# A transformer block of eight batches on one core: a new timetable of filler units and row work, another order of the last batch, and attention output in other PSUM banks

## The chip, the cores and the metric

The kernel runs on one core of a Trainium2 chip. The metric is the device time of one execution in microseconds (us). Three runs of the kernel before gave a median of 995.27 us (992.34 to 995.49).

## The reference

The input x is 8 batches of 512 rows with 256 columns, in fp32. The block does, for each batch:

```
h = layernorm(x) * (1 + ca) + sa                 # ca, sa, ga, sb, cb, gb come from silu(c) @ wmod
x = x + ga * attention(h)
h = layernorm(x) * (1 + cb) + sb
x = x + gb * ffn(h)

attention(h) = light + heavy
light: second layernorm, q, k, v = xl @ wqkv; 8 heads of 64; windows of 64 rows that look at
       themselves and both neighbours; softmax; @ wo_l
heavy: two routers (h @ rt_q, h @ rt_kv) sort the rows; the last 256 of each order are kept;
       rms norm; q = . @ wq_h, k, v = . @ wkv_h; full softmax attention 256 x 256; @ wo_h;
       its rows are set back at the places that the first router picked
ffn(h): y = relu(h @ W_fc^T)^2 @ W_proj^T; five steps of a spiking neuron on y; mean of the spikes
```

## The kernel before, in words

**Slots.** A batch is an iteration of 24 slots. Slots 0 to 15 are light attention, four head pairs p times four row tiles m (s = 4p + m). Slots 16 to 23 are heavy attention, four head pairs times two query tiles. Each slot handles two heads and 128 query rows. Slots are numbered through: n = 24 b + s. The pipeline of one n goes over three engines, written out by hand, and each engine works through them strictly in its written order:

- TensorE in slot n (lines 1094 to 1102): `scores(n+2)`, the slot's filler units, `turn(n)` (six or eight 64-row transposes of the normalized probabilities, line 1053), `attend(n-1)` (the product with v, lines 1074, 1079, 1089).
- VectorE in slot n: `copy_out(n-2)` (line 1323, it evicts the output of attend and adds its two halves; below this is called the eviction), `invert(n+1)` (reciprocal of the row sums, line 1316), `minimum(n+2)` (lines 1306 to 1310), the units' share, then the row work that the function `stages` puts into that slot.
- ScalarE in slot n: `copy_pT(n-1)` (lines 847, 851), `exp_step(n+2)` (line 829), the units' share, `normalize(n+1)` (line 839).

`scores(n+3)` waits for exp of n+2. The attend's output `ps_oT` is columns 256 to 383 of the two banks whose columns 0 to 255 hold the scores (`ps_scores`). Therefore `attend(n-1)` waits for exp of n+2 as well, and `copy_out(n-2)` waits until the scores n+2 are written:

```
ps_oT = ps_scores[:, :, SEL:SEL + P]
pe.wait_ge(exp_ready, min(n + 4, SLOTS * B))       # attend(n)
dve.wait_ge(scores_ready, min(n + 5, SLOTS * B))   # copy_out(n)
```

**Filler units.** The products that aren't attention are cut into units and given to slots by the table `SLOT_UNITS`. HT transposes the routed rows (ScalarE makes the high part, VectorE the low part, line 1342, and frees the bank); Q, K, V, HQ, HK, HV are projections (line 895; fp32 is split in two parts, so there are six matmuls a unit); NQ, NK, NV are those of the next batch; LO (line 943) and HO (line 948) are the two output projections; ZT and Z3 are transposes of normed rows (lines 953, 958); FC and YA (lines 895, 1006) are the feed-forward layer; SR and RK turn the router's scores and count ranks (lines 973 to 982). Units of all kinds but YA use the two banks `ps_unit` in turn, so a unit waits until the one before the last is drained. Heavy output HO, Z3, FC, YA and the neuron work on the batch before: in iteration b they belong to batch b-1.

**Row work on VectorE** (`stages`): statistics and norms of batch b+1 (`stats1`, `center`, `modulate`, `stats2`, `router_scores`, `second_norm`, `compare`), `add_rows`, `stats3`, `third_norm` and ten neuron steps of batch b-1. GpSimd makes reciprocal roots (`rstd1` to `rstd3`), the rms norm (`norm_rows`), the low part of the squares of FC (`square_low`), scatters rows in router order to DRAM (line 619), gathers the heavy output back (line 639), adds x to LO (`add_x`) and ends a batch with `final`. SyncE loads and stores in one fixed order; each of its transfers waits behind all that it issued before.

**The last batch.** Iteration 7 has no next batch to prepare. Its heavy slots come last as in all others, so HO of batch 7, the store of its rows, the gather, `add_rows`, `stats3`, `third_norm`, Z3 and the whole feed-forward layer stand behind them in a segment "tail", which works in two halves of 256 rows.

## Time and profile before

| | |
|---|---|
| median of three runs | 995.27 us |
| the profiled execution | 1000.88 us, with a span of 999.1 us from first to last instruction |
| mean granted TensorE clock | 0.930 of full speed |
| TensorE matmul busy | 855.5 us (86% of the span), 8914 instructions |
| VectorE busy | 556.6 us (56%) |
| ScalarE busy | 583.5 us (58%) |
| GpSimd busy | 396.5 us (40%) |
| starts of slot 0, iterations 0 to 7 | 54.7, 167.1, 276.6, 389.2, 502.0, 614.5, 727.3, 839.8 us |
| chain that ended last | PE 59%, DVE 22%, ACT 8%, issue 6% |

In the profile PE is TensorE, DVE VectorE, ACT ScalarE, POOL GpSimd, SP SyncE. PEclk is the granted TensorE clock as a share of 2.4 GHz; it has two levels, 1.00 and 0.50 (1.2 GHz). L1323 is line 1323 of the kernel.

### The profile page before, as it was taken

Reading aid. Unit: us, or ns where it says so; the run is one execution under the profiler, and the core shown is the slowest. Engines: PE = TensorE matmul, PEld = TensorE weight load, DVE = VectorE, ACT = ScalarE, POOL = GpSimd, SP = SyncE. Lnnn points to the kernel's source line nnn. Section 1 sums busy time; section 2 is a strip of 40 time slices with the busy share of each in tenths; the row PEclk is TensorE's granted clock in tenths of the full one; section 3 lists DMA queues with packets and bytes.
Section 4 is the critical chain, followed back from the end, with each engine's and each line's share of the span. In section 5 each row is a group of like instructions: output and inputs, shape, how many; then the busy total and the mean of one; then the engine's idle time right before and its main releaser. Section 6 shows DMA issues by size and latency. Waiting matters only on the chain.

```text
span 999.1 us, 23412 instructions
## 1 busy us (share of the span) xinstructions
PE 855.5 (86%) x8914; PEld 654.3 (65%) x8914; DVE 556.6 (56%) x1602; ACT 583.5 (58%) x1682; POOL 396.5 (40%) x437
## 2 busy tenths in 40 slices
PE   5758599799988999799988999799988999899655
PEld 2436466577756876577756876577756876587455
DVE  7645634764557554764557554764557554614344
ACT  1156556576656765676656765576556765676332
POOL 3322031375424542365424543365424542252243
PEclk9878779999999999999999999999999999999768
DMA  8220002100210012200220012200220011200100
GB/s 314 67 80 2 27 28 70 59 2 23 80 59 23 2 38 85 59 2 19 71 73 23 1 39 85 60 2 17 72 73 22 3 38 54 59 2 2 37 22 22
DMA packets 32479, 45.33 MB, mean 45 GB/s; under 512 B 3928, under 2 KB 26720, under 8 KB 32368
## 3 DMA queue, kind: packets, MB, share of 16 engines
q1 hardware_dynamic: 26944, 31.24, 9.8%
q0 software_dynamic: 4608, 12.59, 3.8%
q8 instruction: 72, 1.18, 0.5%
q14 instruction: 39, 0.32, 0.1%
q10 hardware_dynamic: 816, 0.00, 0.0%
HBM read 28.85 MB, written 14.97 MB: 44 GB/s over the span
## 4 chain that ended last, share of the span: by engine, by line
PE 59%; DVE 22%; ACT 8%; issue 6%; DMA 2%; POOL 2%; SPq 0%; DVEq 0%; POOLq 0%; ACTq 0%
PE ps_unit L895 25%; PE ps_y L1006 7%; PE ps_unit L943 6%; ACT probs L829 5%; PE ps_unit L948 4%; PE ps_turned L1053 4%; PE ps_scores L1089 3%; PE ps_scores L1074 3%; DVE row_min L1306 3%; PE ps_scores L1038 3%; PE ps_scores L1029 3%; DVE loT L1323 2%; ACT hT L794 1%; DVE bn L1268 1%; DMA late<-in_L_wmod 1%
## 5 line engine op out<-in xcount | busy, mean ns | idle before, releaser
L829 ACT ACTIVATE probs<-ps_scores,row_min 128x192 f32<-128x192 f32 (+2 forms) x384 | 161.3, 425 | 182.8 <-DVE row_min L1306 125.6
L839 ACT ACTIVATE probs<-probs,row_inv 128x192 f32<-128x192 f32 (+2 forms) x384 | 155.7, 458 | 0.0
L1323 DVE TENSOR_REDUCE loT<-ps_scores 128x128 f32<-128x256 f32 x128 | 53.5, 418 | 141.3 <-PE ps_scores L1029 92.0
L895 PE MATMUL ps_unit<-xT,wfcT 128*128 128x512 f32 (+1 forms) x432 | 112.8, 404 | 9.4 <-DVE xT L1247 8.8
L895 PE MATMUL ps_unit<-xT,wqkv 128*128 128x512 f32 x384 | 109.6, 422 | 3.3 <-POOL xT L653 3.3
L1006 PEld LDWEIGHTS ps_y<-wprojT,hid_parts 128*128 128x128 f32 x768 | 99.3, 190 | 9.9 <-issue 6.0
L432 POOL TENSOR_TENSOR hid<-hid 128x512 f32<-128x512 f32 (+1 forms) x64 | 63.5, 992 | 106.4 <-ACT hid L807 105.1
L1006 PE MATMUL ps_y<-wprojT,hid_parts 128*128 128x256 f32 x768 | 104.6, 284 | 0.2
L895 PEld LDWEIGHTS ps_unit<-xT,wfcT 128*128 128x128 f32 x432 | 78.6, 206 | 33.4 <-issue 20.2
L578 POOL TENSOR_SCALAR veps<-mv 128x4 f32<-128x4 f32 (+1 forms) x25 | 5.1, 202 | 227.7 <-DVE mv L1166 133.1
L1074 PE MATMUL ps_scores<-probsT,v 64*64 64x128 f32 x1024 | 58.7, 299 | 38.9 <-ACT probs L829 38.6
L1053 PEld LDWEIGHTS ps_turned<-ident,probs 64*128 64x128 f32 x1280 | 55.6, 140 | 54.9 <-issue 44.3
L895 PEld LDWEIGHTS ps_unit<-xT,wqkv 128*128 128x128 f32 x384 | 71.3, 193 | 24.3 <-issue 10.2
L436 POOL TENSOR_TENSOR hid_parts<-hid,hid_parts 128x512 fp32r<-128x512 f32 (+1 forms) x64 | 79.2, 1237 | 13.4 <-ACT hid_parts L811 11.2
L1053 PE MATMUL ps_turned<-ident,probs 64*128 64x64 f32 x1280 | 82.2, 241 | 1.9 <-ACT probsT L851 1.7
L619 POOL DMA_INDIRECT sorted_rows<-hn,rank x64 | 64.4, 1006 | 45.7 <-DVE rank L1350 33.0
L847 ACT ACTIVATE probsT<-ps_turned 128x384 f32<-128x384 f32 x128 | 61.9, 484 | 33.6 <-PE ps_scores L1079 33.3
L1306 DVE TENSOR_REDUCE row_min<-ps_scores 128x2 f32<-128x512 f32 (+1 forms) x128 | 77.1, 602 | 2.5 <-PE ps_scores L1029 2.5
L1323 DVE TENSOR_REDUCE late<-ps_scores 128x128 f32<-128x256 f32 x64 | 27.0, 422 | 88.0 <-PE ps_scores L1038 44.8
L829 ACT ACTIVATION_READ_ACCUMULATOR probs<-ps_scores,row_min 128x1 f32 x384 | 75.3, 196 | 0.0
L1029 PE MATMUL ps_scores<-kT,qT 64*64 64x192 f32 (+1 forms) x1024 | 71.8, 317 | 3.3 <-ACT probs L829 3.3
L943 PE MATMUL ps_unit<-wo_light,loT 128*128 128x256 f32 x256 | 63.8, 392 | 0.0
(158 smaller groups left out, 1690.9 us busy)
## 6 DMA issues: line engine op xcount, KB each, us to landing
xa<-in_L_attn_x SPq DMA_DIRECT2D x8, 512.0 KB, 5.0
routed<-sorted_rows SPq DMA_DIRECT2D x16, 256.0 KB, 3.0
lx<-in_L_attn_x SPq DMA_DIRECT2D x8, 512.0 KB, 3.8
...
sorted_rows<-hn,rank POOLq DMA_INDIRECT x64, 2.4
...
```

What stands on the lines that cost most here:

```text
L436: eng.tensor_tensor(hid_parts[1][:, i % 2, cols], square, hid_parts[0][:, i % 2, cols].bitcast(F32), ALU.subtract).then_inc(low, 1)
L619: pool.indirect_dma_start(out=sorted_rows[r], out_offset=bass.IndirectOffsetOnAxis(ap=rank[:, r, t:t + 1], axis=0), in_=hn[:, t, :], in_of ...
L829: ins = act.activation(probs[:, probs_buffer(s), probs_columns(s, part)], ps_scores[:, part, lo:hi], ACT.Exp, bias=row_min[:, s % 3, part: ...
L839: ins = act.activation(rows, rows, ACT.Identity, scale=row_inv[:, s % 3, part:part + 1])
L895: ins = pe.matmul(ps, w(wi, k, w_cols), a(ai, k, a_cols), start=(n == 0), stop=(n == 3 * KD - 1))
L943: ins = pe.matmul(ps[:, 0:D], loT[:, p, i * P:(i + 1) * P], wo_light[:, p, :], start=(p == 0), stop=(p == PAIRS - 1))
L1006: ins = pe.matmul(ps_y[t // 2][:, (t % 2) * D:(t % 2 + 1) * D], hid_parts[hi][:, i % 2, t * P:(t + 1) * P], wprojT[wi][:, f, :], start=(f ...
L1029: ins = pe.matmul(ps_scores[c * W:(c + 1) * W, w, lo:hi], qT[heads[h], p % 2, query:query + W], kT[heads[h], p % 2, first_key + lo:first_k ...
L1053: ins = pe.transpose(ps_pT[:, c, i * W:(i + 1) * W], probs[rows, probs_buffer(s), run * P:(run + 1) * P], ident[rows, rows])
L1074: ins = pe.matmul(ps_oT[halves[h], g ^ h, :], v[halves[g], m, cols[h]], both, start=True, stop=m == (T - 1, 0)[g])
L1306: ins = dve.tensor_reduce(row_min[:, s % 3, :], ps_scores[:, :, lo:hi], AX.X, ALU.min)
L1323: dve.tensor_reduce(dst[:, p, m * P:(m + 1) * P], ps_oT.rearrange("p g n -> p n g"), AX.X, ALU.add).then_inc(oT_copied, 1)
```

## The change

It does six things.

1. `ps_oT` moves to columns 256 to 383 of the banks of the turned probabilities (`ps_turned`). `attend` no longer waits for exp. `turn(n)` waits for the eviction of n-2, and the eviction of n waits until the turned probabilities of n+1 are copied. Each row half of attend writes one bank (`g` in place of `g ^ h`).
2. On VectorE the eviction moves behind `invert` and `minimum`.
3. `SLOT_UNITS` is written anew. K(1) moves from the end of the iteration before to slot 0, LO(3) to slot 4 of the next iteration, and SyncE waits for it before gate_a is loaded anew.
4. The row work gets other slots, some of it in two parts (`stats1`, `center`, `stats3`), and the neuron steps go from slots 17 to 20 to slots 20 to 23. GpSimd's steps move with them.
5. Buffers of probabilities and row sums are taken by n, not by s.
6. The last batch has its own order of slots (`LAST_ORDER`) and units (`LAST_UNITS`): light pairs 0 and 1, all heavy slots, then pairs 2 and 3 by row tile. Its heavy output (HX), light output (LX 0, 1), store and gather come inside the iteration, LX(2), LX(3) at the start of the tail.

```diff
 SLOT_UNITS = {
-    0: [("HT", 0), ("V", 3)],
-    1: [("HO", 0), ("HO", 1)],
-    2: [("HT", 1), ("Q", 2)],
-    3: [("HV", 1)],
-    4: [("K", 2)],
+    0: [("HT", 0), ("K", 1), ("HT", 1)],
+    1: [("V", 3), ("HO", 0)],
+    2: [("HO", 1)],
+    3: [("Q", 2)],
+    4: [("K", 2), ("LO", 3)],
     5: [("Q", 3)],
     6: [("K", 3)],
-    7: [("HV", 0), ("Z3", 0), ("Z3", 1)],
-    8: [("FC", 0), ("FC", 1)],
-    9: [("HQ", 0), ("FC", 2), ("YA", 0)],
-    10: [("FC", 3), ("YA", 1), ("SR", 0)],
-    11: [("FC", 4), ("YA", 2)],
-    12: [("FC", 5), ("YA", 3), ("HK", 0)],
-    13: [("RK", 0), ("FC", 6), ("YA", 4), ("SR", 1)],
-    14: [("FC", 7), ("YA", 5)],
-    15: [("YA", 6), ("ZT", 0)],
-    16: [("YA", 7), ("ZT", 1), ("RK", 1)],
-    17: [("HQ", 1), ("HK", 1)],
-    18: [("LO", 0), ("NQ", 0)],
-    19: [("LO", 1), ("NK", 0)],
-    20: [("LO", 2), ("NV", 0)],
-    21: [("LO", 3), ("NQ", 1)],
-    22: [("NV", 1), ("NK", 1)],
-    23: [("NV", 2)],
+    7: [("HV", 1)],
+    8: [("HV", 0)],
+    9: [("Z3", 0), ("Z3", 1), ("HQ", 0)],
+    10: [("HK", 0), ("FC", 0)],
+    11: [("FC", 1), ("SR", 0)],
+    12: [("FC", 2), ("YA", 0)],
+    13: [("FC", 3), ("YA", 1)],
+    14: [("FC", 4), ("YA", 2), ("RK", 0), ("SR", 1)],
+    15: [("FC", 5), ("YA", 3)],
+    16: [("HQ", 1), ("FC", 6), ("YA", 4)],
+    17: [("HK", 1), ("FC", 7), ("YA", 5)],
+    18: [("YA", 6), ("ZT", 0), ("ZT", 1), ("RK", 1)],
+    19: [("YA", 7), ("NQ", 0)],
+    20: [("NK", 0), ("NV", 0)],
+    21: [("LO", 0), ("NV", 1)],
+    22: [("LO", 1), ("NQ", 1)],
+    23: [("LO", 2), ("NV", 2)],
 }
+LAST_ORDER = [*range(LIGHT // 2), *range(LIGHT, SLOTS)] + [p * T + m for m in range(T) for p in (2, 3)]
+LAST_UNITS = {
+    0: [("HT", 0), ("K", 1), ("HT", 1)],
+    1: [("V", 3), ("HO", 0), ("HO", 1)],
+    2: [("HQ", 0)],
+    3: [("HK", 0), ("LO", 3)],
+    4: [("HV", 1)],
+    5: [("HQ", 1)],
+    6: [("HK", 1)],
+    7: [("HV", 0)],
+    8: [("Z3", 0), ("Z3", 1)],
+    9: [("FC", 0), ("Q", 2)],
...
+    18: [("HX", 0), ("HX", 1)],
+    19: [("YA", 6), ("YA", 7)],
+    20: [("LX", 0)],
+    22: [("LX", 1)],
+}
...
-        ps_oT = ps_scores[:, :, SEL:SEL + P]
         ps_turned = ctx.enter_context(nc.psum_tensor("ps_turned", [P, 2, 512], F32))
         ps_pT = ps_turned[:, :, 0:SEL]
+        ps_oT = ps_turned[:, :, SEL:SEL + P]
...
                 pe.wait_ge(probs_ready, n + 1)
-                if not (isinstance(n, int) and n == 0):
+                if n > 0:
                     pe.wait_ge(pT_copied, n)
+                if n > 1:
+                    pe.wait_ge(oT_copied, n - 1)
...
                 if n > 0:
                     pe.wait_ge(oT_copied, n)
-                pe.wait_ge(exp_ready, min(n + 4, SLOTS * B))
...
                 dve.wait_ge(oT_ready, n + 1)
-                dve.wait_ge(scores_ready, min(n + 5, SLOTS * B))
+                dve.wait_ge(pT_copied, min(n + 2, SLOTS * B))
...
-            NEURON = {17: [(0, 1), (0, 2)], 18: [(0, 3), (0, 4), (0, 5)], 19: [(1, 1), (1, 2)],
-                      20: [(1, 3), (1, 4), (1, 5)]}
+            NEURON = {20: [(0, 1), (0, 2)], 21: [(0, 3), (0, 4)], 22: [(0, 5), (1, 1), (1, 2)],
+                      23: [(1, 3), (1, 4), (1, 5)]}
...
                 if not first:
-                    if s == 5:
                     if s == 6:
+                        add_rows(b - 1)
+                        stats3(b - 1, tiles=range(1))
+                    if s == 7:
+                        stats3(b - 1, tiles=range(1, T))
+                    if s == 8:
                         third_norm(b - 1)
...
+                if s == 1:
+                    stats1(b + 1, range(2))
+                if s == 2:
+                    stats1(b + 1, range(2, T))
+                if s in (3, 4):
+                    center(b + 1, range(2 * (s - 3), 2 * (s - 2)))
+                if s == 5:
+                    modulate(b + 1)
+                if s == 10:
+                    stats2(b + 1)
+                    router_scores(b + 1, 0)
+                if s == 11:
+                    router_scores(b + 1, 1)
+                if s in (12, 13):
+                    compare(segment, b + 1, 0, range(2 * (s - 12), 2 * (s - 11)))
+                if s == 14:
+                    second_norm(b + 1)
+                if s in (15, 16):
+                    compare(segment, b + 1, 1, range(2 * (s - 15), 2 * (s - 14)))
...
-                        copy_out(n - 2, (s - 2) % SLOTS)
-                    if not (last and s + 1 >= SLOTS):
-                        invert(n + 1, (s + 1) % SLOTS)
-                    if not (last and s + 2 >= SLOTS):
-                        minimum(n + 2, (s + 2) % SLOTS)
+                        copy_out(n - 2, slot_at(s - 2, last))
...
-            attend("tail", B, SLOTS * B - 1, SLOTS - 1)
+            unit("tail", B, ("LX", 2))
+            attend("tail", B, SLOTS * B - 1, LIGHT - 1)
```

On GpSimd `rstd1` goes from slot 2 to 3, `rstd3` from 5 to 7, `rstd2` from 7 to 10, `norm_rows` from 8 to 11, the scatters from slots 14 to 20 to slots 15 to 21, and the first half of `final` from slot 20 to 23.

## Rows read from the trace of the kernel before

**Rows 1.** Busy time by stretch: two whole iterations; columns stand in the first line.

```profile
core 0: us, PE busy (x) PEld busy (x) DVE busy (x) ACT busy (x) POOL busy (x), PEclk, DMA share, GB/s
167.10:276.60 109.50, 99.77 (x1109) 77.24 (x1105) 66.50 (x193) 70.86 (x207) 50.10 (x53) 0.98 0.13 42
389.20:501.90 112.70, 102.70 (x1110) 79.33 (x1104) 66.53 (x193) 70.79 (x207) 50.35 (x53) 0.95 0.13 40
```

**Rows 2.** Same view, iteration 3: slots 0, 1, 2-8, 9-15, 16-17, 18-23.

```profile
389.20:392.50 3.30, 3.30 (x52) 2.41 (x45) 0.95 (x3) 2.29 (x9) 0.00 (x0) 1.00 0.03 5
392.50:400.50 8.00, 6.42 (x50) 4.85 (x44) 3.27 (x10) 2.61 (x10) 0.00 (x0) 0.79 0.00 0
400.50:431.00 30.50, 23.85 (x266) 16.54 (x261) 22.56 (x77) 18.95 (x58) 11.61 (x17) 0.94 0.17 49
431.00:463.80 32.80, 32.78 (x383) 27.44 (x379) 17.92 (x54) 23.83 (x68) 21.25 (x20) 1.00 0.01 2
463.80:475.50 11.70, 10.14 (x138) 8.80 (x131) 6.77 (x16) 6.77 (x19) 6.55 (x6) 0.85 0.13 46
475.50:501.90 26.40, 26.22 (x274) 19.28 (x270) 15.06 (x34) 16.35 (x48) 10.94 (x11) 1.00 0.29 91
```

**Rows 3.** Same view: slot 1 of iteration 3, and of iteration 1.

```profile
394.90:398.30 3.40, 3.40 (x10) 2.69 (x9) 0.30 (x2) 1.54 (x6) 0.00 (x0) 0.50 0.00 0
169.60:173.10 3.50, 1.93 (x34) 1.50 (x34) 2.33 (x7) 2.10 (x7) 0.00 (x0) 1.00 0.00 0
```

**Rows 4.** Who waited for whom, whole span: us in total, times, longest.

```profile
ACT probs L829 <- DVE row_min L1306: 125.6, 128, 2.8
PE ps_scores L1074 <- ACT probs L829: 38.6, 47, 2.1
```

**Rows 5.** Timeline of slots 0 and 1, iteration 3: start, length, instruction, idle before.

```profile
391.67 0.83 ACT L794 ACTIVATE hT<-ps_unit,gamma_cols 128x256 fp32r<-128x256 f32 x2
392.62 0.87 DVE L1342 SCALAR_TENSOR_TENSOR hT<-ps_unit,gamma_cols,hT 128x256 fp32r<-128x256 f32 x2 [1.79 <-ACT hT L794]
...
394.57 5.38 PE L948 MATMUL ps_unit<-wo_heavy,late 128*128 128x256 f32 x16 [1.58 <-DVE late L1323]
```

**Rows 6.** Busy time by stretch: slot 5 of iteration 3, one unit.

```profile
412.20:415.20 3.00, 2.81 (x43) 1.88 (x36) 2.44 (x7) 2.41 (x10) 0.00 (x0) 1.00 0.00 0
```

**Rows 7.** Costliest groups: the eviction of attention output.

```profile
L1323 DVE TENSOR_REDUCE loT<-ps_scores 128x128 f32<-128x256 f32 x128 | 53.5, 418 | 141.3 <-PE ps_scores L1029 92.0
```

**Rows 8.** Timeline, VectorE, slot 20 of iteration 3: a v copy, three neuron steps.

```profile
488.97 0.69 DVE L1337 COPY v<-ps_unit 128x512 f32<-128x512 f32 x1 [0.98 <-PE ps_unit L895]
489.58 2.13 DVE L1298 SCALAR_TENSOR_TENSOR spikes<-ps_y,spikes 128x512 f32<-128x512 f32 x3
```

**Rows 9.** Timeline of slot 7, iteration 3: Z3 on TensorE and ScalarE.

```profile
423.31 0.66 PE L958 MATMUL ps_unit<-ident,hn 128*128 128x128 f32 x4 [1.55 <-DVE v_r L1337]
...
424.00 0.78 ACT L778 ACTIVATE full<-ps_unit,shift_b,scale_b 128x512 f32<-128x512 f32 x1 [1.43 <-PE ps_unit L958]
```

**Rows 10.** second_norm: all instructions (ns, least/median/most), and those of iteration 3.

```profile
L1216 DVE TENSOR_SCALAR xa<-h,mv,rstd x32: 399/406/1508, 19.5 to 778.8; 128x256 f32<-128x256 f32 x32
...
438.18 3.20 DVE L1216 TENSOR_SCALAR xa<-h,mv,rstd 128x256 f32<-128x256 f32 x4
```

**Rows 11.** DMA issues: count, KB each, median us from issue to landing.

```profile
xa<-in_L_attn_x SPq DMA_DIRECT2D x8, 512.0 KB, 5.0
```

**Rows 12.** Busy time by stretch: slots 8 to 16 of iteration 0.

```profile
90.00:133.50 43.50, 29.23 (x372) 21.51 (x368) 26.58 (x88) 25.15 (x76) 9.09 (x13) 0.75 0.06 20
```

**Rows 13.** By stretch: iteration 7, the way to FC; timeline: Z3 and FC there.

```profile
839.80:936.70 96.90, 87.39 (x997) 66.60 (x986) 41.48 (x116) 64.25 (x189) 31.79 (x31) 0.97 0.08 23
936.70:961.20 24.50, 8.50 (x38) 6.27 (x37) 7.79 (x22) 1.62 (x3) 5.74 (x8) 0.57 0.11 35
...
958.32 1.09 PE L958 MATMUL ps_unit<-ident,hn 128*128 128x128 f32 x4 [12.82 <-DVE hn L1281]
...
961.18 4.04 PE L895 MATMUL ps_unit<-xT,wfcT 128*128 128x256 f32 x18 [1.77 <-DVE xT L1247]
```

More of the change, by code:

```diff
@@ L95, in slot_units, with slot_at @@
 def slot_units(slot, first, last):
[L97 to L98 removed]
+    if last:
+        return LAST_UNITS.get(slot, [])
+    units = [u for u in SLOT_UNITS[slot] if not (first and u in EARLIER_UNITS)]
     return units + FIRST_UNITS.get(slot, []) if first else units
+def slot_at(position, last):
+    return LAST_ORDER[position] if last and 0 <= position < SLOTS else position % SLOTS
 def iteration_units(first, last):
@@ L712, in _ @@
             iteration("last", B - 1, last=True)
-            gather(B - 1, True, in_tail=True)
-            for half in range(2):
-                rstd3(B - 1, half)
+            rstd3(B - 1, 0)
+            add_x("tail", B, ("LX", 2))
+            add_x("tail", B, ("LX", 3))
+            rstd3(B - 1, 1)
             for u in SEGMENTS["tail"]:
-                unit("tail", B, u)
+                if u[0] != "LX":
+                    unit("tail", B, u)
             final(pool, B - 1, 0)
```

256 lines of the change are left out of this document (146 added, 110 removed).

## The prediction

> **What bounds the kernel now.** I read the table by iteration first [rows 1]: how long each is, how much of it TensorE works, at what clock. Iteration 3 lasts 112.7 us, TensorE is busy 102.7 of it, and its granted clock is 0.95; iteration 1 lasts 109.5 with 99.8 busy at 0.98. Iterations 2 to 6 are alike within 0.3 us. The stretches of iteration 3 [rows 2] show where the idle 10.0 us lie: none in slot 0, 1.6 in slot 1, 6.65 in slots 2 to 8, 1.6 in slots 16 and 17, next to none in 9 to 15 and 18 to 23. The clock column there names the second loss: 0.79, 0.94 and 0.85 in the stretches with holes, 1.00 elsewhere. Each is one fall to 1.2 GHz of 3.4 us, as in the first of [rows 3]; the second row there is the same place of iteration 1, where a hole as long brought none. Two falls more cost 102.7 - 99.8 = 2.9 us of busy time, 1.5 each, so a full-clock iteration holds 98.3 us of TensorE work.
>
> The waits [rows 4] name what opens the holes. In a slot VectorE evicts the output of slot n-2, takes the row minimum of n+2, ScalarE makes exp of it, and attend(n-1) waits for that exp, as its output shares the scores' banks: 38.6 us in 47 waits, behind the 125.6 that exp waits for the minimum. The hole of slot 1 is another [rows 5]: HT(0) goes through ScalarE (0.83) and VectorE (0.87, after 1.79 idle) and the eviction that HO(0) needs is queued behind it; TensorE waits 1.58. A slot with one projection is 3.0 us, 2.8 of them work [rows 6]. My split of that 2.8 is 1.3 for the projection and 1.5 for scores, turn and attend; a heavy slot's three take about 1.7. Slots 18 to 23 then leave 26.2 - 7 x 1.3 - 6 x 1.7 = 6.9 for four LO: 1.7 an output unit. All three are estimates from these rows.
>
> **The change, part by part.** *Output into the turned banks.* The attend's wait for exp goes. In its place turn(n) waits for eviction n-2, which VectorE now makes behind the minimum. Scores wait for exp and exp for the minimum, so this loop is one eviction (0.42) [rows 7] shorter: about 0.5 scores, 0.6 minimum, 0.9 exp and gaps, 2.3 us in all. A slot with one unit has 2.84 us of TensorE work, hence it becomes bound by TensorE, if VectorE is on time. The eviction ends 1.6 us after the slot starts and turn comes at 1.8 to 2.0; covered by 0.2 us only. Where VectorE is late, turn is late by the same.
>
> *Timetable of the loop.* Units and VectorE work are the same; TensorE's 98.3 us stay. I walked the new slots, each engine in its order, with the durations above. Slots 1 to 7 come out without holes: every one has a unit, and row work is at most 1.7 us a slot. Four places do not.
> - Slot 0: HT(0), K(1), HT(1), where HT(1) wants the bank of HT(0). VectorE ends slot 23 late: NV(2) is filled 3.6 us into it, the copy takes 0.7, three neuron steps 2.1 [rows 8], so 6.5 against a slot of 4.6. Minimum 0.6, exp 0.8, HT(0) on ScalarE 0.85 and on VectorE 0.9 follow: HT(0)'s bank is free 5.1 us into slot 0, TensorE has had nothing since 2.3. Idle 2.9 with the gaps.
> - Slot 8: HV(1)'s copy and three statistics end 0.9 late, so minimum, eviction and turn: 0.6.
> - Slot 9: Z3 waits for the third norm (0.75), then HQ(0) wants the bank of Z3(0), drained behind exp by a 0.78 activation, as today's 1.55 [rows 9]: 1.35. Together 2.1.
> - Slots 10 and 11: second statistics 1.9 and the router's sums, which GpSimd stretches. Today second_norm, four instructions with a median of 406 ns, takes 3.20 beside GpSimd's squares [rows 10]. So two slots of 4.1 and 3.3 get up to 6 us of VectorE each: 1.0. (The Trainium skill, "SBUF — State Buffer", section Who interferes with whom, says that a VectorE instruction with two SBUF inputs, or in two-port mode, and GpSimd lock each other out for a whole instruction. The trace agrees; by it alone the price would be 0 or 2 as the overlap falls.)
> The rest 0.4. Sum 7.0 against 10.0. The hole before slot 17 closes, as RK(1) has two slots more: no fall there. The holes of slots 0 and 9 are at least as long as those that bring falls today, so two stay, 3.0 us. (The Trainium skill, "TensorE: Matmul & The Clock Gate", section HAM oscillation, tells of falls behind waits for transfers; by its rule holes as short as these would do no harm. Here 1.58 did, so the trace decides; by the page the loop would be 105.3.) A new iteration: 98.3 + 7.0 + 3.0 = 108.3. Six now take 109.5 + 5 x 112.64 = 672.7, then 649.8: **-22.9**.
>
> Transfers move too. final() of the second half now runs on GpSimd 1.9 to 4.4 us into slot 0, and SyncE's store and the load of xa are queued behind it; with 5.0 to land [rows 11] xa comes 10.0 in, the statistics start at 10.8. Cost 0, but 0.8 us of cover; if it goes, the minimum of slot 2 waits, up to 2 us. The gather ends some 22 us in, GpSimd's save_rank and add_x(LO 3) behind it at 23.5, before add_rows at 25. Scatter of the second list ends in slot 21, reload lands 2.6 us before HT(0). All at nothing, bounds 0 and 2 us an iteration for the three.
>
> *First iteration.* 43.5 us of slots 8 to 16 hold 29.2 of TensorE work at a clock of 0.75 [rows 12]: VectorE and the chain bound it. HV(1) leaves slot 3, where its weights are barely made, LO(3) leaves (1.7), K(1) comes behind HT(0). Bounds 0 and -10; I take **-5**, nearer to the moved units' own price than to the idle.
>
> *Last batch.* To its last attend but one it takes 96.9 us, then 24.5 to FC(0) [rows 13]. In those 24.5 TensorE sits 12.8 idle behind HO, store, gather and norm; the row of Z3 shows it, and FC starts at 961.2. Heavy pairs now come before the last eight light slots: HX in slot 18, gather in 19, all below LX and attention. Left behind that attend: LX(2) 1.7, attend 0.7, eviction 0.5, LX(3) 1.7, Z3 0.6, its three steps 2.1 and gaps of 0.4: 7.7. The iteration itself gains the old batch's LO(3), two HX and K(1) and loses its own LO(2) and LO(3): 3 x 1.7 + 1.3 - 2 x 1.7 = 3.0 us, to 99.9. 121.4 - 107.6 = 13.8: **-14**. Bounds -3 (gather late after all) and -17.
>
> Sum -22.9 - 5 - 14 = -42. The profiled execution took 1000.9 (span 999.1 and 1.8 around it), so 958.9; the median shown is 5.6 lower: 953.
>
> **Rivals.**
> *B, holes closed.* ScalarE or VectorE is quicker than I walked, idle 5.5 and no fall: 103.8 an iteration, -49.9 -5 -14: 926. For: the 2.3 us loop, and iteration 1's hole without a fall. Against: the order in slot 0 is fixed by bank and queue. The clock page's rule ends near here, at 935.
> *C, holes only move.* The waits of turn on late evictions eat the rest and three falls stay: loop 112.6, tail -14 and first -5: 976. For: 0.2 us of cover. Against: idle 6.65 in slots 2 to 8 comes from a wait that goes.
> *D, slower.* Each turn waits a full eviction, since VectorE is a slot behind: 0.42 [rows 7] x 190 slots = +80, 953 + 80 = 1033. It needs the wait in more than half of the slots (over 42 us). Against: VectorE is busy 59% of an iteration, and in 12 slots two units cover it.
> *E, the last batch gives nothing* because its gather still ends late: 967.
>
> **How the numbers follow.** A 0.50, B 0.17, C 0.20, E 0.06, D 0.07. The likeliest gives 953. The range runs from 926 (B) to 979 (C and its 3 us), leaving out D and the outer half of B. About 0.3% (3 us) is what a measurement here can tell from none: faster 0.91, same 0.02, slower 0.07.
>
> **What would show it.** Right: attend waits for no exp, 2 to 7 have no idle TensorE, HT(1) waits 2 to 3 us on VectorE, falls in slots 1 and 10 alone, FC of the tail starts within 9 us of the last attend but one. Wrong: turn waiting for VectorE in many slots, xa awaited by VectorE in slot 1, or three falls.

## The result, and the profile after

The changed kernel takes **970.87 us** (median of 4 runs, 969.66 to 971.63); the kernel before, run beside it, 995.38 us (992.34 to 1001.5). The ratio is 0.9745, 95% interval 0.9698 to 0.9792: faster by 2.5%. The forecast was 953.0 us in a range of 926 to 979. The sign and the range hold; the gain is 24.5 us and not 42.

Busy time by stretch, changed kernel: iterations 1 and 3 (columns as in [rows 1]); of iteration 4, slots 0, 1, 2-7, 8-9, 14 and 15; and after the last "..." the last iteration from slot 0 to the end of the last attend but one, and from there to FC(0):

```profile
core 0: us, PE busy (x) PEld busy (x) DVE busy (x) ACT busy (x) POOL busy (x), PEclk, DMA share, GB/s
159.90:265.30 105.40, 100.14 (x1113) 76.81 (x1106) 68.20 (x191) 71.36 (x206) 45.01 (x50) 0.98 0.10 30
375.30:484.40 109.10, 101.41 (x1110) 77.59 (x1104) 70.65 (x194) 71.47 (x206) 49.20 (x54) 0.97 0.13 43
484.40:492.10 7.70, 5.01 (x56) 3.66 (x51) 4.02 (x9) 4.07 (x12) 4.19 (x4) 0.82 0.34 101
492.10:496.70 4.60, 4.60 (x40) 3.30 (x36) 2.60 (x9) 2.23 (x8) 0.00 (x0) 0.93 0.51 149
496.70:515.40 18.70, 18.70 (x233) 13.18 (x229) 13.77 (x43) 14.09 (x46) 6.11 (x8) 1.00 0.22 68
515.40:524.30 8.90, 6.52 (x86) 4.85 (x80) 7.22 (x25) 5.13 (x15) 1.23 (x2) 1.00 0.07 25
...
540.50:548.40 7.90, 6.11 (x84) 4.90 (x80) 6.34 (x13) 5.17 (x14) 5.17 (x5) 0.93 0.00 0
548.40:553.80 5.40, 5.40 (x64) 4.07 (x60) 2.67 (x9) 2.88 (x9) 1.72 (x2) 0.78 0.02 5
...
812.30:916.60 104.30, 93.64 (x1013) 72.37 (x1005) 45.59 (x121) 65.66 (x189) 37.05 (x36) 0.93 0.10 29
916.60:931.20 14.60, 8.07 (x35) 5.90 (x33) 7.58 (x21) 1.62 (x3) 6.74 (x9) 0.73 0.15 45
```

Read it against [rows 1, 2]. Iteration 3 is 3.6 us shorter and its idle is 7.7 us where it was 10.0. In iteration 4 slots 2 to 7 are full: 18.70 busy of 18.70, where slots 2 to 8 left 6.65 us open. What is idle now stands mostly in three places: slot 0 (2.7), slots 8 and 9 (2.4) and slot 14 (1.8). The clock column is below 1 in slots 0-1 and 14-15: two falls to 1.2 GHz of 3.4 us in this iteration, in place of three. The six iterations aren't alike: iteration 1 has 5.3 us of idle and one fall, iteration 2 has three falls and takes 110.1 us, iteration 3 has one fall of 6.8 us, and 4 to 6 have two of 3.4. The last two lines answer to [rows 13].

The waits of the whole span and the eviction's group (columns as in [rows 4] and [rows 7]):

```profile
ACT probs L885 <- DVE row_min L1377: 80.9, 100, 3.5
...
PE ps_turned L1114 <- DVE loT L1394: 16.3, 18, 2.6
```

```profile
L1088 PE MATMUL ps_scores<-kT,qT 64*64 64x192 f32 (+1 forms) x1024 | 73.6, 330 | 3.3 <-ACT probs L885 3.3
L1394 DVE TENSOR_REDUCE loT<-ps_turned 128x128 f32<-128x256 f32 x128 | 53.3, 416 | 10.5 <-ACT probsT L903 9.3
```

Attend's wait for exp, 38.6 us in 47 waits in [rows 4], is gone. The 3.3 us in the row of L1088 are the scores' own wait for exp, which the kernel before has with the same 3.3. In the place of attend's wait stands turn's wait for the eviction, 16.3 us in 18 waits, none of them over 0.5 us in the six loop iterations: 0.48 in slot 8 and 0.38 in slot 13. Before it evicts light output VectorE is idle 10.5 us in all, 9.3 of it for ScalarE's copy of the turned probabilities; before heavy output it waits 0.2 us for it.

By stretches of the span, with the forecast beside them (starts of slots 0 from the first scores of each iteration):

| stretch | before | after | difference | forecast |
|---|---|---|---|---|
| start and first iteration | 167.1 | 159.9 | -7.2 | -5 |
| six loop iterations | 672.7 | 652.3 | -20.4 | -22.9 |
| last iteration and tail | 159.3 | 157.6 | -1.7 | -14 |
| span | 999.1 | 969.8 | -29.3 | -42 |

The profiled run of the kernel before was 5.6 us above its median, that of the changed kernel 0.8 above its own; so 29.3 us of span are 24.5 of median. In the first row 1.6 us lie ahead of slot 0 of iteration 0 (54.66 and 53.04 us) and 5.5 in iteration 0; no run takes these apart.

Slot 0 of iteration 4, in the timeline, answers to [rows 5]:

```profile
485.28 1.65 PE L951 MATMUL ps_unit<-xT,wqkv 128*128 128x512 f32 x6
...
486.29 0.15 DVE L1387 RECIPROCAL row_inv<-row_sum 128x2 f32<-128x2 f32 x1
...
487.74 0.84 ACT L850 ACTIVATE hT<-ps_unit,gamma_cols 128x256 fp32r<-128x256 f32 x2
...
488.69 0.88 DVE L1413 SCALAR_TENSOR_TENSOR hT<-ps_unit,gamma_cols,hT 128x256 fp32r<-128x256 f32 x2 [1.46 <-ACT hT L850]
489.58 0.47 SPq L570 DMA_DIRECT2D xa<-in_L_attn_x  x1
489.62 1.11 PE L980 MATMUL ps_unit<-ident,routed 128*128 128x128 f32 x4 [2.69 <-DVE hT L1413]
```

This is the hole that was forecast. The slot starts at 484.4; VectorE is free of the neuron steps 1.9 us in, HT(0)'s bank is free 5.2 us in (forecast 5.1), and TensorE waits 2.69 us (forecast 2.9 with its gaps).

Slot 14, same view:

```profile
541.60 0.34 DVE L1300 SCALAR_TENSOR_TENSOR late<-late,score,later 128x128 bf16<-128x128 f32 x1
...
542.91 1.35 POOL L481 TENSOR_TENSOR hid_parts<-hid,hid_parts 128x512 fp32r<-128x512 f32 x1
543.04 1.37 DVE L1300 SCALAR_TENSOR_TENSOR late<-late,score,later 128x128 bf16<-128x128 f32 x1
...
544.41 0.67 DVE L1377 TENSOR_REDUCE row_min<-ps_scores 128x2 f32<-128x512 f32 x1
...
545.11 0.47 ACT L885 ACTIVATE probs<-ps_scores,row_min 128x256 f32<-128x256 f32 x1 [2.59 <-DVE row_min L1377]
...
546.02 0.59 ACT L863 ACTIVATE hid<-ps_unit 128x512 f32<-128x512 f32 x1
...
546.67 0.65 PE L1030 MATMUL ps_unit<-ident,score 128*128 128x128 f32 x4 [1.48 <-ACT hid L863]
```

This hole was not forecast. The same instruction of the router's comparison takes 0.34 us at 541.60 and 1.37 us at 543.04, where it starts 0.13 us behind a GpSimd product of 1.35 (the low part of the squares) and ends 0.15 us behind it. So the minimum comes late, exp behind it, and ScalarE drains FC(4)'s bank only behind exp; SR(1) wants that bank. Delays of the kind that I priced in slots 10 and 11 are real, and stand in slots 13 and 14. (The rule of the Trainium skill, "SBUF — State Buffer", section Who interferes with whom, that the prediction tells, agrees with this pair of rows: VectorE's instruction, which started second, ends just behind GpSimd's.)

The way to FC(0) in the last batch, same view:

```profile
908.55 1.40 DVE L1369 SCALAR_TENSOR_TENSOR spikes<-ps_y,spikes 128x512 f32<-128x512 f32 x2
...
908.78 0.40 PE L1114 MATMUL ps_turned<-ident,probs 64*128 64x64 f32 x6 [2.37 <-DVE loT L1394]
...
916.54 3.37 PE L1000 MATMUL ps_unit<-wo_light,loT 128*128 128x256 f32 x8
...
921.32 1.08 DVE L1352 TENSOR_SCALAR hn<-h,mv,rstd 128x256 f32<-128x256 f32 x2 [0.94 <-POOL rstd L627]
922.33 0.41 DVE L1394 TENSOR_REDUCE loT<-ps_turned 128x128 f32<-128x256 f32 x1
922.88 3.60 PE L1000 MATMUL ps_unit<-wo_light,loT 128*128 128x256 f32 x8 [2.48 <-DVE loT L1394]
...
928.57 0.75 DVE L1337 BATCH_NORM_STATS2 bn<-h 128x6 f32<-128x256 f32 x2
...
931.18 1.20 PE L951 MATMUL ps_unit<-xT,wfcT 128*128 128x256 f32 x4 [3.75 <-DVE xT L1313]
```

The gather's wait of 12.82 us is gone, as forecast. But each thing that TensorE still needs is now behind row work on VectorE: the evictions stand behind neuron steps and behind the third norm, which itself waits for GpSimd, and the parts of xT that FC(0) reads stand behind the sums and statistics of the other half. Between these waits the clock falls, and LX(2) and LX(3) take 3.37 and 3.60 us each where run 9's LX(2) takes 1.99 at full clock.

### The profile page after: what moved, and what is told of

Same layout as the page of the kernel before. It is cut to its first block, busy times and chain, and to the rows that moved or that the text cites. A ratio compares the mean times of both kernels' runs of the same rounds, so it can differ in the third digit from the quotient of the medians.

```text
span 969.8 us, 23414 instructions
## 1 busy us (share of the span) xinstructions
PE 853.9 (88%) x8914; PEld 648.3 (67%) x8914; DVE 584.6 (60%) x1602; ACT 589.6 (61%) x1682; POOL 391.0 (40%) x437
## 4 chain that ended last, share of the span: by engine, by line
PE 64%; DVE 19%; ACT 7%; issue 4%; POOL 2%; DMA 2%; SPq 0%; DVEq 0%; ACTq 0%; POOLq 0%
PE ps_unit L951 26%; PE ps_y L1063 7%; PE ps_unit L1000 6%; PE ps_turned L1114 5%; PE ps_turned L1149 4%; PE ps_turned L1134 3%; PE ps_unit L1005 3%; PE ps_scores L1088 3%; PE ps_scores L1097 3%; ACT probs L885 2%; DVE late L1300 2%; DVE late L1297 2%; DVE routed L1273 1%; DVE late L1299 1%; DVE spikes L1369 1%
## 5 line engine op out<-in xcount | busy, mean ns | idle before, releaser
L885 ACT ACTIVATE probs<-ps_scores,row_min 128x192 f32<-128x192 f32 (+2 forms) x384 | 161.7, 426 | 126.2 <-DVE row_min L1377 80.9
L951 PE MATMUL ps_unit<-xT,wqkv 128*128 128x512 f32 x384 | 112.5, 431 | 3.8 <-POOL xT L702 3.8
L1063 PEld LDWEIGHTS ps_y<-wprojT,hid_parts 128*128 128x128 f32 x768 | 99.9, 191 | 9.3 <-issue 5.5
L1114 PEld LDWEIGHTS ps_turned<-ident,probs 64*128 64x128 f32 x1280 | 57.6, 144 | 71.2 <-issue 61.1
L1114 PE MATMUL ps_turned<-ident,probs 64*128 64x64 f32 x1280 | 84.3, 245 | 17.5 <-DVE loT L1394 16.3
L951 PE MATMUL ps_unit<-xT,wfcT 128*128 128x512 f32 (+1 forms) x384 | 95.7, 387 | 4.3 <-DVE xT L1313 3.7
L951 PEld LDWEIGHTS ps_unit<-xT,wfcT 128*128 128x128 f32 x384 | 66.3, 200 | 24.8 <-issue 13.6
L1088 PE MATMUL ps_scores<-kT,qT 64*64 64x192 f32 (+1 forms) x1024 | 73.6, 330 | 3.3 <-ACT probs L885 3.3
L1000 PE MATMUL ps_unit<-wo_light,loT 128*128 128x256 f32 x256 | 67.3, 409 | 2.5 <-DVE loT L1394 2.5
L712 POOL TENSOR_TENSOR lx<-lx,hid 128x256 f32<-128x256 f32 x28 | 20.5, 732 | 102.9 <-DVE hid L1429 102.9
L1134 PE MATMUL ps_turned<-probsT,v 64*64 64x128 f32 x1024 | 60.4, 308 | 0.0
L1000 PEld LDWEIGHTS ps_unit<-wo_light,loT 128*128 128x128 f32 x256 | 49.5, 202 | 16.3 <-issue 9.5
```

The source lines that it names most:

```text
L885: ins = act.activation(probs[:, probs_buffer(n), probs_columns(s, part)], ps_scores[:, part, lo:hi], ACT.Exp, bias=row_min[:, n % 3, part: ...
L951: ins = pe.matmul(ps, w(wi, k, w_cols), a(ai, k, a_cols), start=(n == 0), stop=(n == 3 * KD - 1))
L1000: ins = pe.matmul(ps[:, 0:D], loT[:, p, i * P:(i + 1) * P], wo_light[:, p, :], start=(p == 0), stop=(p == PAIRS - 1))
L1063: ins = pe.matmul(ps_y[t // 2][:, (t % 2) * D:(t % 2 + 1) * D], hid_parts[hi][:, i % 2, t * P:(t + 1) * P], wprojT[wi][:, f, :], start=(f ...
L1088: ins = pe.matmul(ps_scores[c * W:(c + 1) * W, w, lo:hi], qT[heads[h], p % 2, query:query + W], kT[heads[h], p % 2, first_key + lo:first_k ...
L1114: ins = pe.transpose(ps_pT[:, c, i * W:(i + 1) * W], probs[rows, probs_buffer(n), run * P:(run + 1) * P], ident[rows, rows])
```

## The experiments

Twelve kernels ran in three jobs, each beside the kernel before. Each job had another chip, so what differs between jobs may belong to the chip. Ratios are against the kernel before of the same job, with 95% intervals. Loop means the six iterations 1 to 6, end means from the last iteration's slot 0 to the end of the span, both in the profiled execution.

| run | edit | median us | ratio | loop | end |
|---|---|---|---|---|---|
| 1 | bank move alone | 965.93 | 0.9703 (0.9679-0.9727) | 647.3 | 157.3 |
| 2 | the rest, old banks | 978.21 | 0.9822 (0.9793-0.985) | 656.0 | 156.8 |
| 3 | old last batch | 971.64 | 0.9767 (0.9742-0.9793) | 653.3 | 157.1 |
| 4 | HT(1) in slot 2 | 962.71 | 0.9674 (0.9651-0.9698) | 642.2 | 157.1 |
| 5 | norm_rows in slot 14 | 970.46 | 0.9725 (0.967-0.978) | 650.6 | 158.6 |
| 6 | SR(1) in slot 15 | 966.54 | 0.9693 (0.9645-0.9741) | 648.0 | 158.6 |
| 7 | eviction first | 1020.23 | 1.0225 (1.0165-1.0284) | 687.4 | 163.6 |
| 8 | last order on VectorE | 977.12 | 0.9786 (0.9732-0.9841) | 668.0 | 154.5 |
| 9 | changed kernel again | 986.2 | 0.9864 (0.983-0.9899) | 664.9 | 158.3 |
| 10 | bank move alone again | 973.95 | 0.9742 (0.9725-0.976) | 655.1 | 159.8 |
| 11 | as 8, again | 979.55 | 0.982 (0.9778-0.9862) | 662.6 | 151.6 |
| 12 | 4, 6 and 8 together | 962.0 | 0.9629 (0.9609-0.965) | 641.7 | 155.9 |

The kernel before had 995.46 us in the job of 1 to 4, 997.52 in that of 5 to 8, and 999.03 in that of 9 to 12.

The loop of seven of them, taken apart. Busy and idle are TensorE's. The last column is how much of the loop had the granted clock at 0.50. The work is the same in all: TensorE's instruction counts differ by less than 0.1%.

| kernel | loop | idle | busy | at 1.2 GHz |
|---|---|---|---|---|
| before | 672.7 | 59.1 | 613.6 | 54.6 |
| changed | 652.3 | 43.5 | 608.8 | 41.0 |
| run 1, bank move alone | 647.3 | 48.8 | 598.5 | 23.9 |
| run 2, the rest, old banks | 656.0 | 48.6 | 607.4 | 37.6 |
| run 4, HT(1) in slot 2 | 642.2 | 43.7 | 598.5 | 17.1 |
| run 9, changed, other job | 664.9 | 54.4 | 610.5 | 41.0 |
| run 12, 4, 6 and 8 together | 641.7 | 46.4 | 595.3 | 10.2 |

### 1. The bank move alone

The kernel before with `ps_oT` in the turned banks, its waits, and the eviction behind reciprocal and minimum; timetable, row work and last batch as before.

```diff
-        ps_oT = ps_scores[:, :, SEL:SEL + P]
+        ps_oT = ps_turned[:, :, SEL:SEL + P]
...
+                if n > 1:
+                    pe.wait_ge(oT_copied, n - 1)
...
-                pe.wait_ge(exp_ready, min(n + 4, SLOTS * B))
...
-                dve.wait_ge(scores_ready, min(n + 5, SLOTS * B))
+                dve.wait_ge(pT_copied, min(n + 2, SLOTS * B))
```

> The kernel before with part 1 and 2 of the change alone (attention output in the banks of the turned probabilities, eviction behind the minimum), old timetable and old last batch. Theory A (the bank move carries the loop's gain): slots 2 to 8 lose the attend's wait for exp, some 0.3 to 0.4 us in each of seven slots, the holes in slots 1, 7 and 16 stay: 2 to 3 us an iteration, about 978 us. Theory B (the timetable carries it, since VectorE's row work sets the light slots): no change, 993 to 997 us.

Measured: 965.93 us, theory A, with 12 us more than it gave. Of its iteration 4, slots 1, 2-8 and 16-17, as in [rows 2], and the whole:

```profile
491.50:497.90 6.40, 4.75 (x50) 3.68 (x44) 2.95 (x10) 2.28 (x8) 0.00 (x0) 1.00 0.00 0
497.90:526.80 28.90, 23.74 (x266) 16.37 (x260) 22.63 (x78) 18.95 (x58) 11.81 (x17) 0.94 0.18 52
...
559.60:569.10 9.50, 8.56 (x133) 7.26 (x129) 6.85 (x17) 6.54 (x19) 5.30 (x5) 1.00 0.12 43
...
488.20:595.40 107.20, 99.45 (x1112) 76.57 (x1105) 68.73 (x193) 71.26 (x206) 50.80 (x53) 0.98 0.14 43
```

The whole gain of the change is there without the timetable. In this iteration the shorter loop of minimum, exp and attend takes 0.6 us of idle from slots 16 and 17 and 1.5 from slots 2 to 8; the hole of slot 1 is as it was (1.65 and 1.58). Its idle is 107.20 - 99.45 = 7.75 us, as in the changed kernel's iteration 4 (7.7); over the six iterations it is 48.8 against 43.5. Slots 1 and 16-17 are shorter by 1.6 and 2.2 us: their falls are gone, and those 0.6 us of idle. Of three falls an iteration one is left in iterations 2 to 6, in slot 7 or 8.

### 2. The rest alone, with the old banks

```diff
-        ps_oT = ps_turned[:, :, SEL:SEL + P]
+        ps_oT = ps_scores[:, :, SEL:SEL + P]
...
+                pe.wait_ge(exp_ready, min(n + 4, SLOTS * B))
...
-                dve.wait_ge(pT_copied, min(n + 2, SLOTS * B))
+                dve.wait_ge(scores_ready, min(n + 5, SLOTS * B))
```

with the eviction first on VectorE, as before.

> The kernel after with part 1 and 2 undone: new timetable, row work and last batch, but attention output in the banks of the scores, attend waiting for exp and eviction ahead of the minimum. Theory A: slots 2, 3, 5 to 8 and 11, with 2.8 to 3.3 us of work, wait for exp again, 0.3 to 0.5 us each, and the last batch's slots without a unit too: 3 us an iteration and 5 in the last batch, about 995 us. Theory B: within 3 us of the kernel after, 968 to 974.

Measured: 978.21 us, 17 less than before and between the two theories (995 and 968 to 974). Its list of waits has the attend's wait for exp again:

```profile
PE ps_scores L1133 <- ACT probs L885: 25.8, 51, 2.4
```

So the timetable by itself (with the new last batch) gains 17 us, the bank move by itself 30, and both together 24.5. They don't add, and the table of the loop says where. Idle time nearly does: 10.5 us less with the timetable, 10.3 less with the banks, 15.6 less with both. Busy time doesn't: 6.2 less, 15.1 less, and 4.8 less with both. The work being the same, that is the clock.

### 3. The old last batch

The last batch in the old order of slots, with heavy output, store and gather back in the tail, and the tail of the kernel before on each engine. Its units inside the iteration are those of the new `SLOT_UNITS` without the next batch's; the changed loop is kept.

```diff
-LAST_ORDER = [*range(LIGHT // 2), *range(LIGHT, SLOTS)] + [p * T + m for m in range(T) for p in (2, 3)]
+LAST_ORDER = [*range(SLOTS)]
```

> The kernel after with the last batch in the old order: heavy slots last, HO, store, gather and norm in the tail; the rest as after. Theory A (what the profiles' spans say): the new order saves little, since its iteration is longer by more than the moved units; old order costs 2 to 6 us, 973 to 977 us. Theory B (as predicted, the order is worth 14 us, and something else of the last batch lost 12): about 985 us.

Measured: 971.64 us, and 157.1 us for the end where the change has 157.6. Theory B is out, and the cost that theory A gave the old order doesn't show either. The new order of the last batch is worth nothing as it stands.

### 4. HT(1) in slot 2

```diff
-    0: [("HT", 0), ("K", 1), ("HT", 1)],
+    0: [("HT", 0), ("K", 1)],
...
-    2: [("HO", 1)],
+    2: [("HO", 1), ("HT", 1)],
```

> The kernel after with HT(1) in slot 2 instead of slot 0. Theory A (the hole of 2.7 us in slot 0 is the wait for HT(0)'s bank, and the clock's fall there follows from it): both go, 2.7 and 1.5 us an iteration in six or seven iterations, about 945 us. Theory B: the time comes back in slot 2, behind VectorE's copies, or another fall takes its place: 965 to 971 us.

Measured: 962.71 us, between the theories (945, and 965 to 971). Its iteration 4, slot 0, slot 1 and the whole:

```profile
483.30:487.10 3.80, 3.34 (x48) 2.41 (x44) 2.78 (x6) 1.85 (x7) 3.27 (x4) 1.00 0.20 69
487.10:492.50 5.40, 4.46 (x48) 3.30 (x42) 2.94 (x8) 3.49 (x12) 0.96 (x1) 1.00 0.65 188
483.30:589.50 106.20, 98.64 (x1112) 75.80 (x1105) 70.48 (x194) 71.19 (x206) 49.16 (x54) 1.00 0.14 44
```

The iteration's idle is 106.20 - 98.64 = 7.6 us, against 109.1 - 101.4 = 7.7 in the changed kernel. No idle time went. The hole of 2.7 us came apart into 0.5, 0.9 and 1.3 in slots 0, 1 and 3, and what went is the fall behind it and, in this iteration, the other one too: TensorE's busy time is 2.8 us less for the same work, at a clock of 1.00. 98.64 is what I had worked out for an iteration at full clock (98.3). Over the loop it is the same: idle 43.7 us against 43.5, busy 598.5 against 608.8, and 17.1 us at 1.2 GHz where the changed kernel has 41.0. Iterations 4 and 5 have no fall; 2, 3 and 6 keep one or two, in slots 9 and 15.

### 5 and 6. The hole of slot 14

The first moves GpSimd's `norm_rows` from slot 11 to 14, out of the comparison's way; the second gives ScalarE time to drain FC(4) before SR(1) wants its bank.

```diff
-                        if s == 11:
+                        if s == 14:
                             norm_rows(segment, b + 1)
```

> The kernel after with GpSimd's norm_rows in slot 14 instead of 11, so that it no longer runs beside VectorE's compare of slots 12 and 13. Theory A (compare is stretched by GpSimd's use of the shared port, which makes the minimum of slot 14 late and opens the hole of 1.8 us there): compare of slots 12 and 13 gets back to some 0.35 us an instruction, the hole falls to about 0.5 and the clock's fall after it goes: 3 us an iteration less, if the scatters behind norm_rows are hidden: about 953 us. Theory B (the squares do it, not norm_rows): 968 to 972 us.

```diff
-    14: [("FC", 4), ("YA", 2), ("RK", 0), ("SR", 1)],
-    15: [("FC", 5), ("YA", 3)],
+    14: [("FC", 4), ("YA", 2), ("RK", 0)],
+    15: [("SR", 1), ("FC", 5), ("YA", 3)],
```

> The kernel after with SR(1) at the head of slot 15 instead of the end of slot 14. Theory A (1.5 of the 1.8 us idle in slot 14 is SR(1) waiting for the bank that ScalarE drains behind a late exp): that wait goes, TensorE has turn and attend instead, and the fall of the clock with it, 2 to 3 us an iteration: about 955 us. Theory B: turn waits for the late eviction at the same time, the hole stays: 968 to 972 us.

Measured: 970.46 and 966.54 us. The first closes slot 14 in iteration 4 (idle 0.0, 5.4 us long in place of 7.9) and opens 1.2 us more in slot 13; the second leaves no idle in slots 13 and 14 (slot 14 is 4.9 us long). Run 6 shows that the hole was SR(1)'s wait for a bank behind a late exp, as read above.

Run 5's theory A failed: in its trace the second comparison of slot 12 starts at 538.40 us together with the low part of the squares (538.41) and takes 1.43 us, where it took 0.56 beside norm_rows. It is the squares that stretch it, as theory B had it; moving norm_rows only moved them against the comparison. Its time, 970.46, is theory B's as well. Run 8, whose loop is the changed kernel's, ran in the same job: the loops of 5 and 6 are 17.4 and 20.0 us shorter in the profiles, but run 8's profiled execution was the slowest of its four (984.8 against a median of 977.12). By the medians they are 7 and 11 us shorter, with intervals that overlap run 8's, widely for run 5 and barely for run 6. That either makes the kernel faster isn't shown by these two alone.

### 7. The eviction first, with the new banks

```diff
-                    if not (last and s + 1 >= SLOTS):
-                        invert(n + 1, slot_at(s + 1, last))
-                    if not (last and s + 2 >= SLOTS):
-                        minimum(n + 2, slot_at(s + 2, last))
                     if not (first and s < 2):
                         copy_out(n - 2, slot_at(s - 2, last))
+                    if not (last and s + 1 >= SLOTS):
+                        invert(n + 1, slot_at(s + 1, last))
+                    if not (last and s + 2 >= SLOTS):
+                        minimum(n + 2, slot_at(s + 2, last))
```

> The kernel after with VectorE's eviction ahead of reciprocal and minimum again, output still in the banks of the turned probabilities. If the order carries the gain of the bank move (the minimum 0.4 us earlier in each chain-bound slot): slots 2 to 8 and 11 grow by 0.1 to 0.4 us, 980 us. If the attend that no longer waits for exp carries it: within 3 us of 970.9.

Measured: 1020.23 us, slower than before by 2.2% and 40 us beyond the worse of my two forecasts. Its waits, whole span:

```profile
ACT probs L885 <- DVE row_min L1377: 165.6, 125, 3.9
...
DVE loT L1394 <- ACT probsT L903: 105.6, 72, 3.4
DVE late L1394 <- ACT probsT L907: 94.6, 45, 6.7
```

Nothing else differs from the changed kernel, and this order carries the sign of the change. In the turned banks the eviction must wait until ScalarE has copied the turned probabilities of the next slot. Ahead of the minimum it holds VectorE 105.6 + 94.6 = 200 us, where those two waits were 9.3 and 0.2 behind it, and the minimum, exp and turn come late with it: exp waits 165.6 us for the minimum and not 80.9. The length of the wait alone isn't the harm. In the kernel before the eviction also stood first and waited 222 us in all for the scores n+2; but the minimum right behind it needs those same scores, and it doesn't need ScalarE's copy. That last step is argued from the code, not measured by itself. This is rival D's neighbourhood: not a full eviction in every slot, but 49 us over the changed kernel's 970.87 (34 over its 986.2 of run 9).

### 8. The last batch's order on VectorE

```diff
+            copy_out(SLOTS * B - 2, slot_at(SLOTS - 2, True))
             add_rows(B - 1, 0)
             stats3(B - 1, 0)
-            copy_out(SLOTS * B - 2, slot_at(SLOTS - 2, True))
             unit("tail", B, ("LX", 2))
-            third_norm(B - 1, 0)
             copy_out(SLOTS * B - 1, slot_at(SLOTS - 1, True))
+            third_norm(B - 1, 0)
             unit("tail", B, ("LX", 3))
-            add_rows(B - 1, 1)
-            stats3(B - 1, 1)
             for i in range(KD):
                 high_part("tail", B, ("Z3", i))
+            add_rows(B - 1, 1)
+            stats3(B - 1, 1)
```

> The kernel after with another VectorE order at the start of the tail: both evictions ahead of the row work, and the high and low parts of the first Z3 ahead of the second half's add_rows and statistics. Theory A (VectorE's order holds LX(3) back by 1.8 us and FC(0) by 1.6): 3 us less, 968 us. Theory B (TensorE at 1.2 GHz with LX sets this stretch): no change within 1 us.

Measured: 977.12 us, which by itself tells nothing: the end is 154.5 us, 4.1 less than in runs 5 and 6 of the same job, and the loop 668.0, though its code is the changed kernel's with 652.3. The job had no unaltered changed kernel to compare with; the next four have.

### 9. The changed kernel once more

> The changed kernel once more, with nothing altered, beside the next three. In the job of the evictions' order, the statistics' slot and the last batch, slots 5 and 20 of every loop iteration were 0.75 to 0.9 us longer (3.5 to 3.7 and 5.36 us) than in the first profile of the changed kernel (2.75 and 4.41 us), in kernels whose code for these slots is the same. If that belongs to the job and not to the edits, this one shows it too whenever its neighbours do, and its time is 966 to 975 us. If it belongs to the edits, slots 5 and 20 are 2.75 and 4.41 us here and longer in the tail's repeat beside it.

Measured: 986.2 us, 15 more than the same kernel's first measurement; the kernel before moved by 3.6. So the job (or its chip) matters, not the edit. I had expected the longer slots here and got them, but 966 to 975 us for the whole. Its list of waits has entries that the first profile of this kernel has none of:

```profile
DVE row_min L1377 <- remote: 41.1, 10, 5.4
...
DVE row_min L1379 <- remote: 7.6, 3, 4.2
```

The profiles of all eight runs of the second and third job have such waits, and none of the first job's four. At one of the places, the minimum of slot 4, VectorE stands idle 2.25 us where it stood 0.63, and slot 5 is 3.6 to 3.7 us long and not 2.75; slot 20 is 5.4 and not 4.41. The idle of an iteration grows by the two. Over the six iterations the loop is 12.6 us longer, and 10.9 of that is idle; the clock adds nothing on the whole, with 41.0 us at 1.2 GHz in both profiles. Iteration 2 of this run, iteration 4, and its fall of slots 0 to 2:

```profile
270.60:379.50 108.90, 99.09 (x1112) 75.67 (x1108) 70.70 (x194) 71.07 (x206) 49.58 (x54) 1.00 0.14 43
...
488.10:600.70 112.60, 103.09 (x1109) 78.57 (x1104) 70.89 (x194) 71.35 (x206) 49.58 (x54) 0.95 0.13 41
...
492.70:499.50 6.80, 6.19 (x41) 4.63 (x42) 2.39 (x8) 3.62 (x12) 0.13 (x1) 0.50 0.59 176
```

The fall lasts 6.8 us where iteration 4 of the first profile has 3.4 (its iteration 3 has one of 6.8 too). Iteration 2 has 9.8 us of idle, with the hole of 2.7 us in slot 0, and no fall at all. What "remote" stands for is open.

### 10. The bank move alone, again

As run 1.

> The kernel before with the bank move alone, a second time, now beside the changed kernel. Theory 1 (the new timetable costs more in slots 0 and 14 than it saves): again 3 to 8 us below the control, 963 to 968 us. Rival (the first comparison was between two jobs, and the timetable is worth nothing either way): within 2 us of the control.

Measured: 973.95 us, 12.3 below the control, ratios 0.9742 (0.9725 to 0.976) and 0.9864 (0.983 to 0.9899) apart: in this job the bank move alone is faster than the whole change. By how much is less sure. The pauses of run 9 lengthen the loop's idle by 10.9 us over the first profile of that kernel and here by 3.2 over run 1, so much of the 12.3 goes with them; without pauses run 1 is 4.9 us below the changed kernel, with ratios whose intervals overlap.

### 11. The last batch's order, again

As run 8.

> The changed kernel with both last evictions ahead of the row work, and the high parts of the third norm ahead of half 1's sums, a second time. Its first profile had 154.5 us from the last loop iteration's end to the end of the span, where two neighbours of the same job had 158.6 and 158.6, though its whole time was no shorter. Theory 1 (the order on VectorE holds the end of the last batch): again 3 to 5 us less than the control in that stretch, and 966 to 969 us against its 971. Rival (the stretch moves by itself from job to job, and the order is worth nothing): stretch and time within 1 us of the control. That the edit makes the loop slower is a third: loop iterations of 111 to 113 us here and 109 in the control.

Measured: 979.55 us. From the last iteration's slot 0 to the last attend but one, to FC(0), and to the end, first of the control and then of this kernel:

```profile
826.90:932.40 105.50, 92.10 (x1013) 70.68 (x1005) 45.25 (x120) 65.38 (x189) 35.83 (x36) 0.95 0.10 29
932.40:946.60 14.20, 6.55 (x35) 4.52 (x33) 7.75 (x21) 1.62 (x3) 7.02 (x9) 0.88 0.17 46
946.60:985.10 38.50, 25.99 (x196) 25.03 (x196) 17.43 (x34) 13.87 (x34) 13.34 (x18) 0.86 0.05 15
```

```profile
821.50:924.90 103.40, 89.84 (x1014) 69.23 (x1005) 45.21 (x120) 65.40 (x189) 35.88 (x36) 0.98 0.10 29
924.90:934.40 9.50, 6.79 (x35) 4.90 (x33) 7.31 (x17) 1.62 (x3) 5.95 (x7) 0.82 0.27 69
934.40:973.10 38.70, 25.67 (x196) 24.61 (x196) 19.30 (x39) 13.75 (x34) 14.45 (x20) 0.86 0.05 15
```

The step that the edit touches went from 14.2 to 9.5 us with TensorE's work the same, against my 7.7 (3.4 us of the 9.5 are at 1.2 GHz, which makes some 1.7 of the rest); the 2.1 us before it hold a different count of falls and aren't the edit's. The order on VectorE accounts for 4.7 of the 6.5 us by which this step was missed in the job. The whole time's interval overlaps the control's, so the gain of the run as a whole isn't shown, that of the stretch is seen twice.

### 12. Three edits together

Edits 4, 6 and 8.

> The changed kernel with the three edits that each took idle time away: HT(1) in slot 2, SR(1) at the head of slot 15, and the last batch's order on VectorE. Theory 1 (they add, since they act in slots 0, 14 and behind the last loop iteration): loop iterations of 104 to 105.5 us, the last part 154 us, a time of 949 to 957 us. Rival (the clock falls somewhere else, once for every hole that stays, in slots 8 and 9): loop iterations of 106 to 108 us and 959 to 965 us.

Measured: 962.0 us, ratio 0.9629 (0.9609 to 0.965), 24 below the control and 12 below the bank move alone of the same job. It has the lowest ratio here. The loop iterations are 105.3 to 108.1 us, so the rival of this expectation was right and my sum (949 to 957) wrong. Its loop is run 4's (641.7 and 642.2), with 2.7 us more of idle and 3.2 less of busy time. Iteration 4:

```profile
483.60:590.50 106.90, 99.76 (x1110) 77.07 (x1104) 72.09 (x194) 70.48 (x206) 49.67 (x54) 0.98 0.15 43
```

It has 7.1 us of idle, of which what the pauses of slots 4 and 19 leave in slots 5 and 20 makes 1.6 (as in run 9), and a fall in iterations 2, 4 and 6 alone, in slots 9 and 10.

## Why the prediction was right, and where it was not

**Bank move.** Right in kind. Attend waits for no exp, slots 2 to 7 are full, and the cover that I gave turn holds in the loop: two waits of under 0.5 us an iteration. The condition on which rival D rested, VectorE behind by a slot, didn't come. Run 7 shows how near it was, by an order that the change got right.

**Loop, -22.9 forecast, -20.4 measured.** The step "98.3 + 7.0 + 3.0 = 108.3" measured 98.3 to 98.6 of work, 7.7 of idle and two falls: 109.1 in iteration 4. By slots, with the forecast in brackets: slot 0 2.7 (2.9), slot 8 0.5 (0.6), slot 9 1.9 (2.1), slots 10 and 11 none (1.0), slots 13 and 14 2.2 (none). The GpSimd term had the right mechanism and twice too small a size, in the wrong slots: I counted VectorE's own lateness and not the bank that ScalarE drains behind it. The second fall came mostly behind slot 14's hole of 1.8 (iterations 2, 4, 5 and 6), and seldom behind slot 9's of about the same (1 and 2). Both sum to what I took, so the loop's number is partly luck of two errors.

**What the loop's gain is made of.** Here the working misled. It put the gain down to the timetable and the banks together; run 1 shows that the banks alone give as much or more, 25.4 us of loop, and run 10 that they do so again. Put on top of the bank move, the timetable takes 5.3 us of idle out of the loop and pays 10.3 us of busy TensorE for it at the lower clock, 41.0 us at 1.2 GHz in place of 23.9. So it isn't idle time that makes the whole change no faster than its first two parts; it is falls. They are also the larger part of the bank move's own gain: 10.3 us less idle and 15.1 less of busy TensorE for the same work. My rule that "holes as long as those that bring falls today" bring them again failed on run 1: slot 1's hole is the same 1.6 us, and in iterations 2 to 6 its fall is gone. Nor did run 9's iteration 2 fall behind its 2.7. So the length of the one hole before it does not tell whether the clock falls; what does, no run here shows. (The rule of the Trainium skill, "TensorE: Matmul & The Clock Gate", section HAM oscillation, by which I had 105.3 for an iteration without falls, doesn't hold for the changed kernel either: 109.1, with them. It would have been near for run 4: 106.2.)

**First iteration, -5 forecast, -7.2 measured**, inside its bounds. Which of the moved units gave it wasn't tested.

**Last batch, -14 forecast, -1.7 measured.** This is the step that failed, 12.3 us of the span's 12.7. "99.9 to the last attend but one" was 104.3, and "7.7 to FC(0)" was 14.6. The gather did go out of the way. What I had listed behind that attend was TensorE's units, one eviction and the steps of Z3; what I left out is VectorE's queue, in which the row work of half 0 stands ahead of both evictions and that of half 1 ahead of the high parts, and the neuron steps in the slots before. The rows for the neuron steps' durations were in my hands [rows 8]. Run 11 moves the row work, not the neuron steps, and takes 4.7 us off this stretch. The other term that I put at nothing is the clock: between gaps of 1.4 to 2.5 us the short units LX(2) and LX(3) run at half speed. In the iteration itself 14.3 us are at 1.2 GHz where the kernel before has 5.9 in its own; half the difference, 4.2 us, is an estimate of what that costs, beside the 4.4 by which 99.9 was missed. Rival E had this outcome, for a reason that didn't occur.

**The number.** 953 against 970.9 is 12.7 of span (of which the last batch is 12.3) and some 5 of baseline: I subtracted the 5.6 us by which the profiled run of before stood above its median from a kernel that does not show them (0.8).

**Transfers.** The load of xa is issued 5.2 us into slot 0 and the statistics start at 12.2 (forecast 10.8) without a wait of VectorE for it. No wait there charges the moved transfers, as costed.
